# A fused kernel of a state-space block and an FP4 feed-forward: VectorE's order within a turn

## The chip, the cores and the metric

The kernel runs on one core of a Trainium2 chip, in one launch. The metric is the device time in microseconds (us). The core's engines are TensorE (PE, with its weight loads PEld), VectorE (DVE), ScalarE (ACT), GpSimd (POOL) and SyncE (SP, which here only issues transfers). Each runs its own instruction list in order; they meet through semaphores.

## What is computed

With `x` of 2 x 4096 tokens by 512 channels, the result is the sum of `x`, a state-space block and a feed-forward whose operands are quantized to FP4:

```python
xn = layernorm(x)
# state-space block on xn
y  = xn + ssm_scan(rmsnorm(xn, scale1), A, B, C, D)
a  = y + gelu(rmsnorm(y, scale2) @ w1 + b1) @ w2 + b2
# feed-forward on the same xn; q() is blockwise FP4, 16 values to a scale
gate = q(xn) @ q(w_gate).T
up   = q(xn) @ q(w_up).T
f    = q(silu(gate) * up) @ q(w_down).T
out  = x + a + f
```

The hidden width of the feed-forward is 1408 (11 blocks of 128), that of the GELU layer 2048. `q` divides each block of 16 values by its scale, rounds the magnitudes to the eight FP4 values, and multiplies by the scale again.

## The kernel before, in words

Tokens come in 64 tiles of 128, joined to 32 pairs of tiles. A matrix product is done as three passes (high by high, high by low, low by high), for full fp32 accuracy.

**Three stages.** A head (about 0 to 115 us) quantizes and turns the first weights and inputs. Then 179 **turns** of the feed-forward follow, up to about 1780 us (`window(s)`, for s from 1 to `NW` = 179, written out for each engine). Then comes the MLP stage of the GELU layer (`mlp1`, `mlp2`, `gelu_parts`) up to the end. The hidden values of one turn (one hidden block of 128 for two pairs of tiles, 128 partitions by 512) are called group s.

**What a turn does with a group.** In turn s TensorE forms gate(s) and up(s) (`gu_half`, line 752), 12 matmuls each, and down(s-2) (`down`, line 774), 12 matmuls. ScalarE takes SiLU of gate(s) into the one buffer `sg` (line 1326). Everything else of turn s is about group s-1, a chain across three engines: VectorE multiplies `sg` by up's bank (`h_mult`, line 957), turns 32x32 blocks so that the 16-value blocks lie along the row (`h_rows`, line 965), reduces and inverts the scales (`front`: lines 992, 1003, 997); GpSimd multiplies by the inverse (`scaled`, line 1527); ScalarE takes magnitudes (line 1291); VectorE rounds in two passes (`mid_a` and `mid_b`, lines 1009 and 1017); GpSimd multiplies by the scale (`dequant`, line 1533); VectorE turns the blocks back (`h_back`, line 971); ScalarE rounds to the high part (line 1319) and GpSimd subtracts it (`h_low`, line 1541). down(s-1) reads that in turn s+1.

**The order by hand.** Each engine's list is written out. The waits that matter here: up(s) may overwrite its bank only after `h_mult(s-1)` (line 751, semaphore `s_hm`); gate(s) only after SiLU(s-1); SiLU(s) may overwrite `sg` only after `h_rows(s-1)` (line 1325); `h_mult(s)` waits for SiLU(s) and up(s) (lines 955 and 956); `down(s)` waits for `h_low(s)` (line 767). On VectorE, `h_mult(s-1)` is the first step of turn s, and `h_back(s-1)` all but the last.

**Side work in a turn.** In some turns VectorE also quantizes another tile (a "side job", `SIDE`): `x_norm` (line 978), which waits for a load, and `front` in one turn, `mid_a`/`mid_b` in the next, and an `x_turn` (line 1032) behind `h_back` two turns after that. Others have statistics (`stats`), sums of finished output tiles (`z_add`, line 1119), taps of the state-space kernel (turns 11 to about 65) or the state-space matmuls (`ssm_*`, turns 99 to 162).

**The normed tiles.** From turn 164 (`PRE0`) on, the first four tiles of the MLP stage are prepared in three steps each (`prepare(t, part)`): part 0 is `tile_add` (lines 1181 and 1185; it waits for the loads of lines 570 and 574), part 1 `tile_root` (lines 1191, 929 to 945, and 1197), part 2 `tile_low` (line 1212). On VectorE parts 1 and 2 stand ahead of the rounding passes, part 0 behind the turn's last step. SP issues the loads of tile 0 behind its turn 163, those of tile t+1 behind TensorE's `h_turn(t)` (line 857). GpSimd adds two sums to each tile (`tile_z`, lines 1618 and 1621), the second behind part 0. In turns 176 to 179 VectorE also splits weights (`w_low`, line 1176), behind `h_back`.

Of the kernel before, what the change touches and what calls it, by code (L numbers as in the profile page):

```python
# [24 lines left out]
NW = NP // 2 * NF + LAG  # L25
NV = 32
NB = NT // 4
SW = 1
# [3 lines left out]
PRE0 = 164  # L32
# [16 lines left out]
def last(n):  # L49
    return first(n) + NF - 1  # L50
# [39 lines left out]
def side(s):  # L90

    return JOF[SIDE[s]] if s in SIDE else None


def prompt(m):

    return SWIN[JOBS[m]] < NF


def h_job(s):  # L100

    return JOF["h", s - 1] if SW <= s <= NW else None
# [31 lines left out]
def plan_slice(s):  # L134

    def upto(s):
        if s < UW0:
            return 0 if s < SW else min(s, 4) if s < 8 else min(s - 3, NT - 4)
        return NT - 4 + min(NT, 2 * (s - UW0 + 1))
    return range(upto(s - 1) if s else 0, max(upto(s), upto(s - 1) if s else 0))  # L140
# [18 lines left out]
def job_width(m):  # L159
    kind, i = JOBS[m]  # L160
    if kind == "h":
        return 2 * P * len(pairs(i))
    return CW[(i - 22) // 4] if kind == "w" and i >= 22 else 512


def build(nc, x, A, B, C, Dv, sc1, sc2, w1, b1, w2, b2, wg, wu, wd, cst, out):
# [12 lines left out]
    with ExitStack() as ctx:  # L179
# [735 lines left out]
        def vector_program(e):  # L915
# [37 lines left out]
            def h_mult(w):  # L953
                n = job_width(JOF["h", w])
                e.wait_ge(s_sg, w + 1)
                e.wait_ge(s_gu, w + 1)
                e.tensor_tensor(sg[:, 0:n], UB_[:, 0:n], sg[:, 0:n], ALU.mult).then_inc(s_hm, 1)  # L957

            def h_rows(w):

                m = JOF["h", w]
                n = job_width(m)
                wait_qa(e, m)
                e.wait_ge(s_hm, w + 1)
                e.transpose(qa[:, m % 4, 0:n], sg[:, 0:n]).then_inc(s_src, 1)  # L965

            def h_back(w):
                m = JOF["h", w]
                n = job_width(m)
                e.wait_ge(s_ph, m + 1)  # L970
                e.transpose(qb[:, m % 2, 0:n], qa[:, m % 4, 0:n]).then_inc(s_t2, 1)  # L971
# [9 lines left out]
            def biggest(m):  # L981
                n = job_width(m)
                s_ = qs[:, m % 4, 0, 0:n // 16]
                if JOBS[m][0] == "w" and m < NJ:
                    e.wait_ge(d_xin[NLOAD[m] % 4], 16 * (NLOAD[m] // 4 + 1))
                elif JOBS[m][0] == "w":
                    e.wait_ge(d_xs[place(m)], 16 * loads(m))
                else:
                    e.wait_ge(s_src, NSOURCE[m])
                if m >= 4:  # L990
                    e.wait_ge(s_ph, m - 3)
                e.tensor_reduce(s_, blk(job_in(m)), AX, ALU.max, apply_absolute_value=True).then_inc(s_mx, 1)  # L992

            def inverse(m):
                nb = job_width(m) // 16
                e.wait_ge(s_sc, m + 1)
                e.reciprocal(qs[:, m % 4, 1, 0:nb], qs[:, m % 4, 0, 0:nb]).then_inc(s_rc, 1)  # L997

            def front(m):
                s_ = qs[:, m % 4, 0, 0:job_width(m) // 16]  # L1000
                biggest(m)
                e.wait_ge(s_mx, m + 1)
                e.tensor_scalar(s_, s_, 1.0 / 6.0, 1e-12, ALU.mult, ALU.max).then_inc(s_sc, 1)
                inverse(m)
# [14 lines left out]
            def low(m):  # L1019
                nk = job_width(m) // P  # L1020
                hi, lo = job_dst(m)
                tin = turned(m).rearrange("p (k c) -> p k c", c=P)
                e.wait_ge(s_hi, TPOS[m])
                e.tensor_tensor(lo, tin, hi.bitcast(F32), ALU.subtract).then_inc(s_lo, 1)  # L1024

            def x_turn(m):

                n = JOBS[m][1] // 2
                e.wait_ge(d_xb[place(m)], 64 * returns(m))
                if n >= 3:  # L1030
                    e.wait_ge(s_gu, last(n - 3) + 1)
                e.transpose(whole(m), xin[:, place(m)].rearrange("p (k c) -> p k c", c=P)).then_inc(s_xt, 1)
# [69 lines left out]
            def ssm_scan(v, h):  # L1102
                w = 2 * v + h
                e.wait_ge(s_e, 2 * v + 2)
                if w:
                    e.wait_ge(s_sb, w)
                else:
                    e.wait_ge(d_a128, 16 * 32)
                    e.wait_ge(d_uo[0], 16 * 8)
                    e.wait_ge(d_uo[1], 16 * 8)  # L1110
                for k in range(4):
                    ins = e.tensor_tensor_scan(sS[:, k, :], a128[:, w:w + 1].to_broadcast([P, 32]),
                                               SSB[0][:, P * h + 32 * k:P * h + 32 * k + 32], 0.0, ALU.mult, ALU.add)
                ins.then_inc(s_scan, 1)

            def z_add(t):
                e.wait_ge(s_dn, last(t // 2) + 1)
                e.wait_ge(d_xr[t % 2], 16 * (t // 2 + 1))
                e.tensor_tensor(xin[:, 2 + t % 2], DNB[t % 4][:], xin[:, 2 + t % 2], ALU.add).then_inc(s_z, 1)
# [3 lines left out]
            def window(s):  # L1123
                k = s - S0
                h, x_ = h_job(s), side(s)
                fronted, low_x = side(s - 1), side(s - 3)
                outputs = 0 <= k < 2 * NV and k % 2
                h_mult(s - 1)
                if low_x in TPOS:
                    low(low_x)  # L1130
                elif low_x is not None and prompt(low_x):
                    x_turn(low_x)
                h_rows(s - 1)
                front(h)
                if outputs:
                    ssm_scan(k // 2, 0)
                for n in range(NP):
                    if s == last(n) + 3:
                        z_add(2 * n)
                        z_add(2 * n + 1)  # L1140
                for n in plan_slice(s):
                    kind, t = LATER[n]
                    if kind == "bn":
                        stats(t)
                    if kind == "bn" and t + 1 == ROOTS[rooted(t) - 1][1]:
                        todo.extend(batch_rsqrt(rooted(t) - 1))
                for step in todo[0:6 if s < 14 else 3]:
                    step()
                del todo[0:6 if s < 14 else 3]
                if PRE0 <= s < PRE0 + 12 and (s - PRE0) % 3 == 1:  # L1150
                    prepare((s - PRE0) // 3, 1)
                if PRE0 + 3 <= s < PRE0 + 15 and (s - PRE0) % 3 == 0:
                    prepare((s - PRE0) // 3 - 1, 2)
                if outputs:
                    ssm_scan(k // 2, 1)
                if fronted is not None:
                    mid_a(fronted)
                    mid_b(fronted)
                mid_a(h)
                mid_b(h)  # L1160
                if s in (K0 - 2, K0 - 1):
                    kernel_heads(s - K0 + 2)
                if x_ is not None:
                    if SIDE[s][0] == "x":
                        x_norm(x_, place(x_), lambda: e.wait_ge(d_xs[place(x_)], 16 * loads(x_)))
                    front(x_)
                h_back(s - 1)
                if low_x in XPOS and not prompt(low_x):
                    x_turn(low_x)
# [47 lines left out]
            def prepare(t, part):  # L1217
                if t < NT:
                    (tile_add, tile_root, tile_low)[part](t)
# [21 lines left out]
            for m in range(NJ + 2):  # L1241
                if m < NJ:
                    if HEAD[m][0] == "x":
                        x_norm(m, m % 4, lambda: e.wait_ge(d_xin[NLOAD[m] % 4], 16 * (NLOAD[m] // 4 + 1)))
                    biggest(m)
                if m >= 2:
                    mid_a(m - 2)
                if m < NJ:
                    inverse(m)
                if m >= 2:  # L1250
                    mid_b(m - 2)
                if m < 2:
                    stats(2 * m)
                    stats(2 * m + 1)
                if m == 1:
                    steps.extend(batch_rsqrt(0))
                for step in steps[0:2]:
                    step()
                del steps[0:2]
            for s in range(SW, NW + 1):  # L1260
                window(s)
                if PRE0 <= s < PRE0 + 12 and (s - PRE0) % 3 == 0:
                    prepare((s - PRE0) // 3, 0)
                if 0 <= s - (NW - 3) < 4:
                    w_low(s - (NW - 3))
            gelu_parts(0)
# [438 lines left out]
```

## Time and profile before

| | |
|---|---|
| median of 3 runs | 3181.51 us (3181.39 to 3181.73) |
| the profiled execution | 3186.95 us |
| its span | 3185.2 us |
| TensorE busy | 3076.3 us, 97% |
| VectorE busy | 2016.9 us, 63% |
| ScalarE, GpSimd busy | 1090.9 us, 1152.1 us |

All rows come from one profiled execution; its own time is 5.4 us above the median, and 1.75 us of it lie outside the span. A row of the timeline gives start, duration, engine, line, operation, the tiles written and read with their shapes, the count of merged instructions, and in square brackets the idle time of the engine just before, with what ended it. For merged rows the duration is that of the whole run.

### The profile page before, as it was taken

To read this page: it belongs to the slowest core of one execution; us is meant where nothing else is said; L and a number is where in the kernel's file an instruction comes from. 1 tells how busy PE (TensorE), PEld (TensorE's weight loads), DVE (VectorE), ACT (ScalarE), POOL (GpSimd) and SP (SyncE) were. 2 spreads that over 40 slices of the span, in tenths; PEclk is the share of its full clock that TensorE was granted. 3 is DMA by queue.
4 is the path that set the end of the run, shared out by engine and by line. 5 is a ranking of instruction groups with operands and counts; after the bars stand their busy time and mean duration, and the time that the engine had idled before them with its cause. 6 is when DMAs were issued, how large, how long until landed. Compare 5 with 4: busy or idle time off the path is not lost.

```text
span 3185.2 us, 43122 instructions
## 1 busy us (share of the span) xinstructions
PE 3076.3 (97%) x14861; PEld 2470.3 (78%) x14861; DVE 2016.9 (63%) x4427; ACT 1090.9 (34%) x1910; POOL 1152.1 (36%) x1097
## 2 busy tenths in 40 slices
PE   5799999999999999999999999999999999999999
PEld 2578777777777777777777788888888888888887
DVE  7788888887777666766777654444454544454442
ACT  5435655545444333334332322121222121122121
POOL 7555556555555545555554211110111111111100
PEclk9999999999999999999999999999999999999999
DMA  4133333347766665666643533333333333333320
GB/s 119 47 87 90 111 118 90 107 119 178 186 175 161 160 166 144 157 161 176 159 117 91 136 70 72 74 71 78 65 80 73 70 71 74 71 70 75 71 59 15
DMA packets 865577, 335.58 MB, mean 105 GB/s; under 512 B 680400, under 2 KB 771792, under 8 KB 862800
## 3 DMA queue, kind: packets, MB, share of 16 engines
q1 hardware_dynamic: 865360, 332.83, 42.8%
q8 instruction: 119, 1.95, 0.2%
q14 instruction: 98, 0.80, 0.1%
HBM read 225.21 MB, written 107.51 MB: 104 GB/s over the span
## 4 chain that ended last, share of the span: by engine, by line
PE 64%; DVE 18%; issue 6%; POOL 4%; ACT 3%; DMA 2%; SPq 2%; DVEq 0%; ACTq 0%; POOLq 0%
PE bank L874 22%; PE bank L890 22%; PE bank L752 11%; PE bank L774 5%; DVE qs L992 3%; POOL qa L1533 3%; DVE qa L1009 2%; DVE qa L965 2%; DVE sg L957 2%; PE bank L815 2%; DVE qb L1017 2%; POOL qa L1527 1%; ACT ub L1378 1%; PE bank L823 1%; DVE qb L971 1%
## 5 line engine op out<-in xcount | busy, mean ns | idle before, releaser
L874 PE MATMUL bank<-hT,Wp 128*128 128x512 f32 x3072 | 743.6, 391 | 2.1 <-DVE Wp L1176 1.6
L890 PE MATMUL bank<-Wp,G 128*128 128x512 f32 x3072 | 743.8, 391 | 0.0
L874 PEld LDWEIGHTS bank<-hT,Wp 128*128 128x128 f32 x3072 | 576.4, 188 | 127.8 <-issue 2.0
L890 PEld LDWEIGHTS bank<-Wp,G 128*128 128x128 f32 x3072 | 576.6, 188 | 126.2
L752 PE MATMUL bank<-XT,Wu 128*128 128x512 f32 (+1 forms) x2148 | 522.3, 392 | 39.7 <-DVE sg L957 38.5
L752 PE MATMUL bank<-XT,Wg 128*128 128x512 f32 (+1 forms) x2148 | 525.5, 394 | 12.8 <-DVE Wd L1024 5.8
L774 PE MATMUL bank<-Wd,HT 128*128 128x512 f32 x2112 | 514.0, 392 | 0.4 <-POOL HT L1541 0.4
L752 PEld LDWEIGHTS bank<-XT,Wu 128*128 128x128 f32 x2148 | 397.7, 190 | 147.5 <-issue 68.2
L1225 DVE CAST G<-gf 128x512 fp32r<-128x512 f32 x256 | 110.3, 431 | 607.5 <-PE bank L890 588.4
L752 PEld LDWEIGHTS bank<-XT,Wg 128*128 128x128 f32 x2148 | 398.5, 190 | 103.0 <-issue 14.6
L774 PEld LDWEIGHTS bank<-Wd,HT 128*128 128x128 f32 x2112 | 393.7, 188 | 94.0 <-issue 12.3
L1533 POOL TENSOR_TENSOR qa<-qb,qs 128x512 f32<-128x512 f32 (+2 forms) x277 | 306.7, 1108 | 319.2 <-DVE qb L1017 316.8
L1479 ACT ACTIVATE gf<-bank,vec 128x512 f32<-128x512 f32 x256 | 176.2, 688 | 613.8 <-PE bank L874 613.8
L1527 POOL TENSOR_TENSOR qa<-qa,qs 128x512 f32<-128x512 f32 (+1 forms) x243 | 263.2, 1083 | 209.3 <-DVE qs L997 209.3
L1618 POOL TENSOR_TENSOR zx<-zl,b2r 128x512 f32<-128x512 f32 x64 | 86.7, 1355 | 615.2 <-DMA out_dram<-zx 532.3
L1541 POOL TENSOR_TENSOR HT<-qb,HT 128x512 fp32r<-128x512 f32 (+1 forms) x179 | 229.7, 1283 | 194.4 <-ACT HT L1319 194.4
L1621 POOL TENSOR_TENSOR zx<-zx,xl 128x512 f32<-128x512 f32 x64 | 82.9, 1295 | 515.4 <-DVE xl L1185 515.3
L1319 ACT ACTIVATE HT<-qb 128x512 fp32r<-128x512 f32 (+1 forms) x179 | 112.1, 626 | 381.0 <-DVE qb L971 380.9
L971 DVE STREAM_TRANSPOSE qb<-qa 128x512 f32<-128x512 f32 (+1 forms) x179 | 122.0, 682 | 137.6 <-POOL qa L1533 137.6
L1227 DVE TENSOR_TENSOR G<-gf,G 128x512 fp32r<-128x512 f32 x256 | 186.2, 728 | 8.8
L1326 ACT ACTIVATE sg<-bank 128x512 f32<-128x512 f32 (+1 forms) x179 | 105.9, 591 | 244.5 <-PE bank L752 198.9
L1009 DVE SCALAR_TENSOR_TENSOR qa<-qb,qa 128x512 f32<-128x512 f32 (+2 forms) x149 | 116.1, 779 | 93.3 <-ACT qb L1291 93.0
(114 smaller groups left out, 2840.4 us busy)
## 6 DMA issues: line engine op xcount, KB each, us to landing
px<-in_L_attn_x_dram SPq DMA_DIRECT2D x128, 256.0 KB, 3.2
xin<-in_L_attn_x_dram SPq DMA_DIRECT2D x128, 256.0 KB, 3.4
sT<-r_K SPq DMA_DIRECT2D x128, 256.0 KB, 4.1
r_Z<-xin SPq DMA_DIRECT2D x64, 256.0 KB, 2.3
r_U<-ub SPq DMA_DIRECT2D x16, 1024.0 KB, 6.6
sU<-r_U SPq DMA_DIRECT2D x32, 512.0 KB, 5.4
r_Y<-sY SPq DMA_DIRECT2D x16, 1024.0 KB, 5.5
xl<-in_L_attn_x_dram SPq DMA_DIRECT2D x64, 256.0 KB, 3.1
```

The lines of the kernel that those rows point to most:

```text
L752: ins = e.matmul(bk[:, 0:n], W[wh][:, k, :], inputs(xh, w, k), start=(k == 0 and p_ == 0), stop=(k == KD - 1 and p_ == 2))
L774: ins = e.matmul(DNB[t % 4][:], HT[hh][:, w % 2, a * P:(a + 1) * P], Wd[wh][:, f, :], start=(w == first(n) and p_ == 0), stop=(w == last(n ...
L874: ins = e.matmul(bk[:], Wp[f][wh][:, 0, k * P:(k + 1) * P], hT[xh][b % 2][:, k, :], start=(k == 0 and p_ == 0), stop=(k == KD - 1 and p_ = ...
L890: ins = e.matmul(ACC[j][:], G2[gh][:, n % 2, j * P:(j + 1) * P], Wp[f][wh][:, 1, :], start=(f == 0 and p_ == 0), stop=(f == 15 and p_ == 2))
L971: e.transpose(qb[:, m % 2, 0:n], qa[:, m % 4, 0:n]).then_inc(s_t2, 1)
L1009: e.scalar_tensor_tensor(Aa, Bb, FLOOR, Aa, ALU.max, ALU.add).then_inc(s_t, 1)
L1227: e.tensor_tensor(G2[1][:, n % 2], gf[:, n % 2], G2[0][:, n % 2].bitcast(F32), ALU.subtract).then_inc(s_glo, 1)
L1319: e.activation(HT[0][:, w % 2, 0:n], qb[:, m % 2, 0:n], ACT.Copy).then_inc(s_hh, 1)
L1479: e.activation(gf[:, n % 2], PB[n % 2][:], ACT.Gelu, bias=vec[:, f:f + 1]).then_inc(s_gl, 1)
L1527: e.tensor_tensor(blk(qa[:, m % 4, 0:n]), blk(job_in(m)), bc(qs[:, m % 4, 1, 0:n // 16], n // 16), ALU.mult).then_inc(s_pa, 1)
L1533: e.tensor_tensor(blk(qa[:, m % 4, 0:n]), blk(qb[:, m % 2, 0:n]), bc(qs[:, m % 4, 0, 0:n // 16], n // 16), ALU.mult).then_inc(s_ph, 1)
L1541: e.tensor_tensor(lo, qb[:, m % 2, 0:n], hi.bitcast(F32), ALU.subtract).then_inc(s_hl, 1)
```

## The change

On VectorE alone:

- `h_mult(s)` moves from the first step of turn s+1 to a place ahead of `h_back(s-1)` in turn s. So the product of the next group comes before the last group is turned back. The product of group 0 stands ahead of the loop.
- Part 0 of a normed tile moves from behind the turn to the place where parts 1 and 2 stood; parts 1 and 2 move behind the rounding passes (and behind a side job's `x_norm` and `front`), just ahead of the product.

```diff
--- before.py
+++ after.py
@@ -1125,7 +1125,6 @@
                 h, x_ = h_job(s), side(s)
                 fronted, low_x = side(s - 1), side(s - 3)
                 outputs = 0 <= k < 2 * NV and k % 2
-                h_mult(s - 1)
                 if low_x in TPOS:
                     low(low_x)
                 elif low_x is not None and prompt(low_x):
@@ -1147,10 +1146,8 @@
                 for step in todo[0:6 if s < 14 else 3]:
                     step()
                 del todo[0:6 if s < 14 else 3]
-                if PRE0 <= s < PRE0 + 12 and (s - PRE0) % 3 == 1:
-                    prepare((s - PRE0) // 3, 1)
-                if PRE0 + 3 <= s < PRE0 + 15 and (s - PRE0) % 3 == 0:
-                    prepare((s - PRE0) // 3 - 1, 2)
+                if PRE0 <= s < PRE0 + 12 and (s - PRE0) % 3 == 0:
+                    prepare((s - PRE0) // 3, 0)
                 if outputs:
                     ssm_scan(k // 2, 1)
                 if fronted is not None:
@@ -1164,6 +1161,12 @@
                     if SIDE[s][0] == "x":
                         x_norm(x_, place(x_), lambda: e.wait_ge(d_xs[place(x_)], 16 * loads(x_)))
                     front(x_)
+                if PRE0 <= s < PRE0 + 12 and (s - PRE0) % 3 == 1:
+                    prepare((s - PRE0) // 3, 1)
+                if PRE0 + 3 <= s < PRE0 + 15 and (s - PRE0) % 3 == 0:
+                    prepare((s - PRE0) // 3 - 1, 2)
+                if s < NW:
+                    h_mult(s)
                 h_back(s - 1)
                 if low_x in XPOS and not prompt(low_x):
                     x_turn(low_x)
@@ -1257,10 +1260,9 @@
                 for step in steps[0:2]:
                     step()
                 del steps[0:2]
+            h_mult(SW - 1)
             for s in range(SW, NW + 1):
                 window(s)
-                if PRE0 <= s < PRE0 + 12 and (s - PRE0) % 3 == 0:
-                    prepare((s - PRE0) // 3, 0)
                 if 0 <= s - (NW - 3) < 4:
                     w_low(s - (NW - 3))
             gelu_parts(0)
```

No instruction is added or removed, and the lists of the other engines stay as they are.

## Rows read from the trace of the kernel before

**Rows 1.** The page: busy time, share of the span, instructions.

```profile
PE 3076.3 (97%) x14861; PEld 2470.3 (78%) x14861; DVE 2016.9 (63%) x4427; ACT 1090.9 (34%) x1910; POOL 1152.1 (36%) x1097
```

**Rows 2.** The busy time by stretch (start:end and length, then PE, PEld, DVE, ...).

```profile
1900.00:3185.00 1285.00, 1281.87 (x5610) 1052.48 (x5608) 598.74 (x1562) 253.18 (x565) 140.81 (x107) 1.00 0.33 68
```

**Rows 3.** TensorE's waits, whole span: total us, times, longest.

```profile
PE bank L752 <- DVE sg L957: 38.5, 43, 2.9
...
PE bank L752 <- issue: 4.5, 2, 2.7
```

**Rows 4.** The same view by stretch: 200 to 1010, then 1640 to 1785 us.

```profile
PE bank L752 <- DVE sg L957: 21.0, 30, 1.6
...
PE bank L752 <- DVE sg L957: 10.4, 9, 2.9
```

**Rows 5.** Timeline, a turn in which VectorE waits ahead of turning back.

```profile
415.32 0.69 DVE L1017 SCALAR_TENSOR_TENSOR qb<-bank,qa 128x512 f32<-128x512 f32 x1
...
416.09 1.06 POOL L1533 TENSOR_TENSOR qa<-qb,qs 128x512 f32<-128x512 f32 x1 [1.65 <-DVE qb L1017]
417.18 0.71 DVE L971 STREAM_TRANSPOSE qb<-qa 128x512 f32<-128x512 f32 x1 [1.17 <-POOL qa L1533]
...
418.41 0.65 DVE L957 TENSOR_TENSOR sg<-bank,sg 128x512 f32<-128x512 f32 x1
...
418.64 1.29 POOL L1541 TENSOR_TENSOR HT<-qb,HT 128x512 fp32r<-128x512 f32 x1 [1.49 <-ACT HT L1319]
...
419.21 2.98 PE L752 MATMUL bank<-XT,Wu 128*128 128x512 f32 x12 [0.64 <-DVE sg L957]
...
422.02 2.91 PE L774 MATMUL bank<-Wd,HT 128*128 128x512 f32 x12
```

**Rows 6.** Timeline, a turn with a side job ahead of turning back.

```profile
426.67 0.66 DVE L971 STREAM_TRANSPOSE qb<-qa 128x512 f32<-128x512 f32 x1
...
427.24 0.65 DVE L957 TENSOR_TENSOR sg<-bank,sg 128x512 f32<-128x512 f32 x1
```

**Rows 7.** Timeline, TensorE rows released by the product.

```profile
123.57 1.66 PE L752 MATMUL bank<-XT,Wu 128*128 128x256 f32 x12 [0.45 <-DVE sg L957]
...
216.40 3.00 PE L752 MATMUL bank<-XT,Wu 128*128 128x512 f32 x12 [1.03 <-DVE sg L957]
...
1237.06 4.38 PE L752 MATMUL bank<-XT,Wu 128*128 128x512 f32 x12 [2.93 <-DVE sg L957]
...
1761.79 2.49 PE L752 MATMUL bank<-XT,Wu 128*128 128x256 f32 x12 [2.93 <-DVE sg L957]
```

**Rows 8.** Timeline, a load waited for, and TensorE released by GpSimd's last subtraction.

```profile
1233.90 0.55 DVE L978 TENSOR_SCALAR qa<-xin,mv,rst 128x512 f32<-128x512 f32 x1 [6.17 <-DMA xin<-in_L_attn_x_dram]
...
966.55 3.02 PE L774 MATMUL bank<-Wd,HT 128*128 128x512 f32 x12 [0.37 <-POOL HT L1541]
```

**Rows 9.** Timeline, normed tile 0: scales, add, product, then steps of the root.

```profile
1643.92 0.35 DVE L997 RECIPROCAL qs<-qs 128x32 f32<-128x32 f32 x1
...
1650.51 0.86 DVE L1181 TENSOR_SCALAR xl<-xl,mv,rst 128x512 f32<-128x512 f32 x1
...
1652.01 0.68 DVE L957 TENSOR_TENSOR sg<-bank,sg 128x512 f32<-128x512 f32 x1
...
1655.09 0.10 DVE L1191 TENSOR_SCALAR rs<-rs 128x1 f32<-128x1 f32 x1
...
1655.26 1.06 POOL L1527 TENSOR_TENSOR qa<-qa,qs 128x512 f32<-128x512 f32 x1 [0.51 <-DVE qs L997]
1655.42 0.91 DVE L933 TENSOR_TENSOR rs<-rs 128x1 f32<-128x1 f32 x1
...
1657.92 0.49 DVE L1197 TENSOR_SCALAR xl<-xl,rs 128x512 f32<-128x512 f32 x1
```

**Rows 10.** Line 574 from 1643.5 to 1645 us: tile 0's second load alone.

```profile
L574 SPq DMA_DIRECT2D yl<-r_Y x1: 1907/1907/1907, 1643.0 to 1643.0; - x1
DMA to landing us min/median/max: 5.1/5.1/5.1
```

## The prediction

> **What bounds the kernel now.** I read the page first: TensorE is busy for 97% of the span and VectorE for 63% [rows 1]. So TensorE sets the time, and only its idle time of 3185.2 - 3076.3 = 109 us can be won. The busy time by stretch comes next: from 1900 us to the end TensorE is busy for 1281.87 of 1285 us [rows 2], so the MLP stage holds nothing, and the change doesn't touch it. TensorE's waits then say who ends the idle time: the largest item is the product of gate and up, line 957, with 38.5 us in 43 waits of at most 2.9 us [rows 3]. That is the wait of up(s) for the product of group s-1, which the change moves. Most of the rest lies in the head ahead of the turns, where there is no product yet. By stretch the 38.5 us are 21.0 in the turns from 200 to 1010 us (30 waits) and 10.4 in the last turns (9) [rows 4]; of the other four, two lie between, in the state-space stage, with 2.93 each (the later one at 1237.06), and two in the first turns, with 1.2 together [rows 7].
>
> The timeline shows what VectorE does ahead of such a product, and there are two kinds. **Kind A**: VectorE ends its second rounding pass at 416.01, waits 1.17 us for GpSimd's scale, turns the group back, does another turning, and starts the product at 418.41; TensorE had stood for 0.64 us [rows 5]. I count 25 of these, the first at 216.40 and the last at 1761.79 [rows 7], 22.8 us together: 16 of them with 12.4 us in the stretch of 21.0, all nine of the stretch of 10.4. **Kind B**: a side job fills that wait, so turning back starts at once and the product 0.57 us behind it [rows 6]. These are 18, first 123.57 and last 1237.06 [rows 7], with 38.5 - 22.8 = 15.7 us.
>
> **The change part by part.** No instruction is added or removed.
>
> *The product ahead of turning back.* In kind A it can start at about 416.05 in place of 418.41, 2.3 us earlier, since its up(s) ended long before (TensorE is already standing ahead of up(s+1)). Its 0.65 us then lie in the 1.17 us in which VectorE waited for GpSimd, so the turning back isn't later, and the next turn's chain starts about 0.6 us earlier. The longest wait of kind A before 1640 us is 1.6 us, under 2.3, so all 16 go: 12.4 us. In kind B the product comes 0.57 us earlier and nothing else does: turning back slips by 0.6 us, `h_rows` stays. Cut by 0.57 at most, the 14 of kind B from 200 to 1010 us (8.6 us in all, seven of them above 0.57) give 7 x 0.57 + 2.4 = 6.4 us.
>
> *What comes back.* Where two such turns follow each other, the second wait grows by what the first lost, because VectorE's own chain is no faster through a turn of kind B: four such places, some 1.3 us. At 202.95 and 233.30 us gate waits with no releaser named (4.5 us, rows 3), and there GpSimd's subtraction of a turned tile ends just before it; that hangs on VectorE's chain, not on the product, and takes back about 0.7 us of what two earlier waits lose. The 1.2 us of the first two turns I take as lost again, since TensorE next waits there for VectorE's low part of a weight. So the stretch to 1010 us gives 12.4 + 6.4 - 1.3 - 0.7 = 16.8 us.
>
> *The two waits of 2.93 us in the state-space stage* are of kind B with a load in front: VectorE stood 6.17 us for an input tile [rows 8]. The load's time stays; each gives 0.57, together 1.1 us.
>
> *Normed tiles.* Gross there are 10.4 us [rows 4]. Against them stands the new order. Part 0 of tile 0 now comes when VectorE gets past its scales, at 1643.92 + 0.35 = 1644.3 [rows 9], but the second load lands only at 1643.0 + 5.1 = 1648.1 [rows 10]. So VectorE stands 3.8 us with the rounding passes of both a side job and the group behind it; GpSimd's scale, ScalarE's high part and TensorE's down wait behind those. By my count the product of that turn then ends at about 1653.1, where it ended at 1652.01 + 0.68 = 1652.7 before [rows 9], and the next turn's chain starts 1.3 us late. For tiles 1 to 3 the load costs 0 to 3 us, mostly in slack. The root takes 1655.09 to 1658.41, 3.3 us [rows 9]. Before it lay partly in VectorE's wait for ScalarE's magnitudes; now it stands bare ahead of the product, and only the 1.1 us of GpSimd's scale cover it for the turning back. So in each of the four turns with a root the product is about as late as before, and behind `tile_add` GpSimd's two sums meet its subtraction. The low part (1.1 us) fits under the scale. Won is the 1.5 us that `tile_add` stood ahead of the product (1650.51 to 1652.01, rows 9). Following the eleven turns row by row, I get between 1 us and 4 us for them and the last turns with `w_low`, where the product no longer stands behind the weight split (2.93 us at 1761.79, rows 7). Bounds: all 10.4 at best; at worst 3 us lost, a wait of 1.8 more in each root turn. I take 2, near the row count.
>
> *The product beside GpSimd.* It now runs while GpSimd scales. The trace has no such pair for line 957, but a two-input pass with one operand in PSUM, 415.32, takes 0.69 us [rows 5], the shortest of such passes; I take 0. The bound is 1.06 us, GpSimd's own duration, from below 0.
>
> *The rule on ports.* A root step of one element that started 0.16 us behind GpSimd's 1.06 us took 0.91 us [rows 9]; a few more of the moved steps now meet GpSimd. The Trainium skill, SBUF — State Buffer, section Who interferes with whom, says that VectorE's instructions with two SBUF inputs, and its two-port modes, exclude GpSimd's reads for their whole length, either way round. By that rule both parts of `tile_add` would also meet the scaling with the inverse, up to 1.06 us in each of four turns, and the sum would be 16 us in place of 20. By that rule also the product, with one operand in PSUM, stays free; no row of it shows the contrary.
>
> **The sum.** 16.8 + 1.1 + 2 = 19.9, say 20 us. The profiled execution would take 3186.95 - 20 = 3167.0; the median of the runs stands 5.4 us lower, so 3161.5 us.
>
> *The clock* I leave out of the sum. Behind the waits of 2.93 us the twelve matmuls of up took 4.38 us [rows 7], and 2.98 us behind one of 0.64 [rows 5]. If the shortened 2.35 us don't bring that, up to 1.4 us more are won at each; 2.35 lies between the two rows, nearer to the longer, so I count nothing.
>
> **Rivals.**
> (1) *All product waits go*, if TensorE's lead never meets another wait, and the clock stays up: 38.5 us, 3143 us. For it: 2.3 us of room in kind A. Against: kind B gains only 0.57, loads and roots stay. 10%.
> (2) *The next wait takes over.* down(s-1) needs GpSimd's subtraction, which ended at 418.64 + 1.29 = 419.93, 2.1 us ahead of down at 422.02 [rows 5]; as TensorE gets earlier, this room shrinks, and once it was already used up (0.37 us at 966.55, rows 8). With the turned tiles of `x_turn` it is the same. Half of the 17.9 us before 1640 comes back, and the normed tiles give nothing: 9 us, 3172.5 us. 20%.
> (3) *Slower: the product holds the turning back.* `h_back` now stands behind a product that waits for up(s). Where VectorE is ahead of TensorE, the group is turned back only 0.65 us after up(s) ends, then ScalarE, GpSimd and down(s-1) follow. It decides from the point at which turning back is later than the 2.1 us of room. ScalarE's magnitudes come behind SiLU(s), which needs gate(s), so the passes end close to the end of up(s) and nothing should be held. Were it 0.25 us beyond the room in each of the 179 turns, 45 us would come and 20 go: 3206 us. 6%.
> (4) *No measurable change*, if roots and load waits (up to 3 us a tile) eat what is won: within 6.4 us, 3180. 8%.
> The forecast, a gain of 14 to 28 us, has the remaining 56%.
>
> **How the numbers follow.** A measurement can tell about 0.2% (6.4 us) from no change. Faster is the forecast with (1) and (2), 86%; same (4), 8%; slower (3), 6%. The range goes from 3146 us (a gain of 35, short of rival 1) to 3174 us, with most of rival 2 inside; outside are the far end of (1), (3) and (4), not quite 2 in 10.
>
> **What would show it.** TensorE's wait for line 957 falls from 38.5 to about 15 us: near 0 for turns without a side job, about 2.35 twice, 1 to 2 in root turns. VectorE's wait for line 1533 ahead of line 971 (1.17 each) shrinks to about 0.5. A new wait of 3 to 4 us for `yl` stands ahead of line 1185 at tile 0. Rival 2 would show as waits for line 1541 or with no releaser; rival 3 as VectorE idle ahead of line 957 for TensorE's line 752 in most turns. The forecast is wrong if the product's waits go and the time doesn't follow.

## The result, and the profile after

The changed kernel takes **3164.52 us** (median of 4 runs, 3164.18 to 3165.86) against 3181.62 (4 runs, 3181.39 to 3182.23): ratio 0.9939, 95% interval 0.9927 to 0.9952. By the medians that is 17.1 us less, by the ratio 19 us; the time is 3 us above the forecast of 3161.5 and inside its range.

The page of after, against [rows 1]:

```profile
span 3162.4 us, 43122 instructions
PE 3064.0 (97%) x14861; PEld 2470.7 (78%) x14861; DVE 2046.9 (65%) x4427; ACT 1088.3 (34%) x1910; POOL 1147.0 (36%) x1097
```

The span is 22.8 us shorter: 10.5 us of TensorE's idle time are gone (108.9 to 98.4) and 12.3 us of its busy time. VectorE is 30 us *busier*, with the same instructions. TensorE's waits over the turns, against [rows 3]:

```profile
PE bank L752 <- DVE sg L957: 16.8, 19, 2.2
PE bank L752 <- DVE Wd L1024: 6.3, 4, 2.3
PE bank L774 <- POOL HT L1543: 6.0, 7, 1.4
PE bank L815 <- DVE sS L1112: 5.3, 6, 1.1
PE bank L752 <- issue: 5.2, 2, 3.4
```

The product (line 957) gave up 21.7 of its 38.5 us. Some 12 us of waits came back at other places, though: before, the low part (line 1543, 1541 before) had 0.4 us in one wait, the state-space scan's copy (line 1112) 0.4 in two, `Wd` 5.8 in four, and the waits with no releaser 4.5 [rows 3 for the last]; the waits behind the feed-forward turns add 0.5. By stretch it is now 6.3 us in 11 waits from 200 to 1010 us, and 5.6 us in 5 from 1640 to 1785 [against rows 4].

Sorted by whether turn s-1 has a side job, the waits of up(s) for the product are these. Kind A (no side job) went from 22.8 us in 25 waits to 6.1 in 6, and none of the six comes before turn 165. Kind B went from 15.7 us in 18 to 10.7 in 13.

To see where the time comes from I compare the start of up(s), turn by turn, and call the difference the **lead** over before. It is 6.8 us at turn 28, 16.8 at turn 61, 24.1 at turn 102, 24.0 at turn 161, 25.1 at turn 177 (1761.79 [rows 7] less 1736.70), and 22.8 at the end. So the gain is made in the plain feed-forward turns, nothing moves in the state-space stage, and the end gives 2.3 back. The lists of TensorE's waits hold only part of it. Of the 24.0 us from turn 0 to turn 102, 13.9 are idle time and 10.1 are *busy* time. In 60 of these turns neither kernel has a listed wait, and they gained 6.7 us; the other 42 gained 17.3 us, where their listed waits fell by 13.3. Gaps under 0.15 us, which no list shows, can't be the difference: they sum to 1.2 us before and 0.7 after. Nor can the clock: the granted clock is 1.00 in this stretch in both kernels. The rest stands in the matmul records, whose ends are modelled. The weight loads (PEld) show it, as in turn 51 before:

```profile
560.97 2.57 PEld L752 LDWEIGHTS bank<-XT,Wu 128*128 128x128 f32 x12 [0.54 <-issue]
561.00 2.96 PE L752 MATMUL bank<-XT,Wu 128*128 128x512 f32 x12
```

The matmuls have no wait, but their weight load stood 0.54 us until the product's end (560.86). The turn took 8.57 us before and 8.16 after, where that idle time is gone. Over the whole run the idle time of these loads with no releaser ("issue") fell from 68.2 to 26.5 us.

What VectorE did with the cover. The turn of [rows 5] is now:

```profile
408.76 0.68 DVE L957 TENSOR_TENSOR sg<-bank,sg 128x512 f32<-128x512 f32 x1
408.93 1.06 POOL L1535 TENSOR_TENSOR qa<-qb,qs 128x512 f32<-128x512 f32 x1 [1.65 <-DVE qb L1017]
410.02 0.71 DVE L971 STREAM_TRANSPOSE qb<-qa 128x512 f32<-128x512 f32 x1 [0.57 <-POOL qa L1535]
```

The product lies in GpSimd's scale, and of VectorE's wait of 1.17 us ahead of turning back 0.57 are left. Over the whole run, first that wait, before and after (total, times, longest), then the scale step, line 1003, before and after (out<-in, count, busy us, mean ns, idle before).

```profile
DVE qb L971 <- POOL qa L1533: 137.6, 114, 2.2
```

```profile
DVE qb L971 <- POOL qa L1535: 55.7, 106, 1.6
```

```profile
L1003 DVE TENSOR_SCALAR qs<-qs 128x32 f32<-128x32 f32 x234 | 49.3, 211 | 8.1
```

```profile
L1003 DVE TENSOR_SCALAR qs<-qs 128x32 f32<-128x32 f32 x234 | 96.5, 413 | 8.1
```

VectorE saves 81.9 us of waiting, and pays 47.2 us of it back in an instruction that nobody touched. Of its 234 executions 13 took over 0.35 us before, 98 after. The turn of [rows 6] shows why; the first two rows are of before, the others of after:

```profile
428.06 1.30 POOL L1541 TENSOR_TENSOR HT<-qb,HT 128x512 fp32r<-128x512 f32 x1 [0.17 <-ACT HT L1319]
...
429.47 0.18 DVE L1003 TENSOR_SCALAR qs<-qs 128x32 f32<-128x32 f32 x1
```

```profile
418.70 0.63 DVE L957 TENSOR_TENSOR sg<-bank,sg 128x512 f32<-128x512 f32 x1
419.24 0.70 DVE L971 STREAM_TRANSPOSE qb<-qa 128x512 f32<-128x512 f32 x1
419.86 0.67 DVE L965 STREAM_TRANSPOSE qa<-sg 128x512 f32<-128x512 f32 x1
420.57 0.69 DVE L992 TENSOR_REDUCE qs<-qa 128x32 f32<-128x512 f32 x1
420.69 1.29 POOL L1543 TENSOR_TENSOR HT<-qb,HT 128x512 fp32r<-128x512 f32 x1 [0.77 <-ACT HT L1321]
421.29 0.73 DVE L1003 TENSOR_SCALAR qs<-qs 128x32 f32<-128x32 f32 x1
422.05 0.35 DVE L997 RECIPROCAL qs<-qs 128x32 f32<-128x32 f32 x1
```

The product no longer stands between turning back and the blocks of the next group. Before, the scale step started 2.80 us behind the start of the turning back (426.67, rows 6), 0.11 us after the end of GpSimd's low part. Now it starts 2.05 us behind, while GpSimd makes the low part of the last group, which begins 1.45 us behind the turning back and lasts 1.29. It ends at 422.02, as GpSimd's instruction does (421.98). The search for the maxima, beside the same instruction, takes its usual 0.69 us. This is the exclusion that the prediction weighed for other instructions. The Trainium skill (SBUF — State Buffer, Who interferes with whom) has VectorE's second port pair shared with GpSimd under an exclusive lock; the trace agrees, with 0.18 us free and 0.73 us beside it.

### The profile page after: what moved, and what is told of

Read it like the earlier page. It is cut to its first block, busy times and chain, and to the rows that moved or that the text cites. A ratio compares the mean times of both kernels' runs of the same rounds, so it can differ in the third digit from the quotient of the medians.

```text
span 3162.4 us, 43122 instructions
## 1 busy us (share of the span) xinstructions
PE 3064.0 (97%) x14861; PEld 2470.7 (78%) x14861; DVE 2046.9 (65%) x4427; ACT 1088.3 (34%) x1910; POOL 1147.0 (36%) x1097
## 4 chain that ended last, share of the span: by engine, by line
PE 69%; DVE 14%; issue 5%; POOL 4%; DMA 3%; SPq 2%; ACT 2%; DVEq 0%; POOLq 0%; ACTq 0%
PE bank L874 22%; PE bank L890 22%; PE bank L752 14%; PE bank L774 7%; DVE qs L992 2%; POOL qa L1535 2%; DVE qa L1009 2%; PE bank L815 2%; DVE qs L1003 1%; DVE qa L965 1%; DVE qb L1017 1%; POOL qa L1529 1%; PE bank L823 1%; PE bank L722 1%; SPq L493 1%
## 5 line engine op out<-in xcount | busy, mean ns | idle before, releaser
L752 PE MATMUL bank<-XT,Wu 128*128 128x512 f32 (+1 forms) x2148 | 513.6, 388 | 17.1 <-DVE sg L957 16.8
L752 PEld LDWEIGHTS bank<-XT,Wu 128*128 128x128 f32 x2148 | 399.8, 189 | 106.9 <-issue 26.5
L992 DVE TENSOR_REDUCE qs<-qa 128x32 f32<-128x512 f32 (+1 forms) x243 | 165.2, 680 | 8.3
```

The lines of the kernel that those rows point to most:

```text
L752: ins = e.matmul(bk[:, 0:n], W[wh][:, k, :], inputs(xh, w, k), start=(k == 0 and p_ == 0), stop=(k == KD - 1 and p_ == 2))
```

## The experiments

Ratios are against the kernel before on the same chip (3184 to 3186 us there); "worth" is the ratio's difference from 1 times 3182 us. no_cover, side_turns, plain_turns, side_last, low_later and rows_too are built on product_only; steps_only, product_first and add_behind on the changed kernel. The cuts of code are shortened: the product of group 0 ahead of the loop and lines that only move are left out, and the remarks behind # are not in the kernels.

**Does a repeat read the same?** One run of the kernel before, unchanged, and the changed kernel again.

> The kernel before, unchanged, for a second profile of it. Theory 1 (the profile of before was a usual one): its span again stands some 3.7 us above the median of the runs, and TensorE waits again 38 to 39 us for the product. Theory 2 (that execution was slow by 5 us somewhere): a span of about 3180 us, and the places where the two profiles of the same kernel differ hold the 5 us; then part of the 22.8 us between the two spans is not the change's.

> The changed kernel, unchanged, beside the others on this chip. Both theories: 0.994 of before (0.993 to 0.995), and its profile again shows about 17 us of product waits, 6 us of waits of down for GpSimd's subtraction and 5 us of the state-space outputs for the scan.

The kernel before took 3187.73 us, product waits 39.0 us in 41, lead never over 1 us at the turns named above. The changed kernel took 3164.01 us, ratio 0.9935 (0.9923 to 0.9948), lead 23.8 at turn 102 and 25.5 at turn 177. So the first profile of before was a usual one, and at these turns two executions of one kernel agree to about 1 us; over the whole span the changed kernel's two profiles are 1.6 us apart. Between kernels it can be more. product_only (below) has the changed kernel's order up to turn 163, and leads by 20.2 us at turn 102, not 24; its profiled execution was the slowest of its five. So a difference of under 4 us between the leads of two kernels tells nothing; what a lead gains between two turns of one execution is read below, to about 1 us.

**The two parts of the change alone.** product_only moves the product and leaves the steps of the normed tiles; steps_only does the reverse.

```diff
-                h_mult(s - 1)            # first step of turn s
+                if s < NW:               # ahead of h_back(s - 1)
+                    h_mult(s)
```

> Only the product is moved; the steps of the normed tiles stay where they were. Theory 1 (the product makes the gain, the steps' move gives nothing or costs a little): 3161 to 3164 us, as fast as the changed kernel or up to 3 us faster, and TensorE's waits for GpSimd's subtraction (line 1543) of the last turns are gone. Theory 2 (the steps' move is worth its own 2 us or more): 3167 us or more.

> Only the steps of the normed tiles are moved; the product stays the first step of a turn. Theory 1: 3180 to 3186 us, no faster than before: what the add no longer holds up, the root now holds up, since it stands bare behind the rounding passes. Theory 2 (the steps are worth something by themselves): 3174 to 3178 us.

product_only: 3160.73 us, ratio 0.9924 (0.9911 to 0.9936), worth 24 us. steps_only: 3192.34 us, 1.0017 (1.0008 to 1.0026), a loss of 5 us; its lead falls from 0.9 at turn 161 to -7.0 at turn 177. The product carries the whole gain. That the steps cost some of it rests on steps_only, whose interval lies above 1, and on the leads; the intervals of product_only and the changed kernel overlap.

**What in the product's move pays?** no_cover keeps the new order and takes the cover away; VectorE waits for GpSimd's scale first:

```diff
                 if s < NW:
+                    e.wait_ge(s_ph, JOF["h", s - 1] + 1)
                     h_mult(s)
```

> Product alone moved, as in product_only, but VectorE first waits for GpSimd's scale, so that the product stands ahead of turning back and is no longer covered by that wait. Theory 1 (in turns without a side job half of the gain comes from the cover: the product starts 1.2 us later than in product_only and every chain through such a turn is 0.65 us longer): gain of 9 to 14 us of the 24, that is 3172 to 3177 us where before is 3186. Rival (the order alone makes the gain, for most waits are under 0.7 us): 20 us or more.

It was slower than before: 3195.45 us, ratio 1.0035 (1.0023 to 1.0048), where I expected a gain. The timeline of no_cover: the wait has moved to the product, with the turning back behind both, and in the next turn (last row) the scale step is blocked as in after.

```profile
417.74 0.69 DVE L957 TENSOR_TENSOR sg<-bank,sg 128x512 f32<-128x512 f32 x1 [1.17 <-POOL qa L1536]
418.35 0.70 DVE L971 STREAM_TRANSPOSE qb<-qa 128x512 f32<-128x512 f32 x1
...
429.62 0.73 DVE L1003 TENSOR_SCALAR qs<-qs 128x32 f32<-128x32 f32 x1
```

Line 1003 is blocked 98 times of 234, as in after, so the new order by itself is worth less than nothing (-11 us). The whole gain hangs on the 0.65 us of VectorE's work that lie in GpSimd's time.

**Which turns pay?** side_turns moves the product only in turns with a side job, plain_turns only in the others.

```diff
-                if s < NW:
+                if s < NW and x_ is not None:     # side_turns; plain_turns: x_ is None
                     h_mult(s)
...                                   # in the other turns h_mult(s - 1) opens the turn, as before
```

> The product ahead of turning back only in turns with a side job (kind B); in all others it stays the first step of the next turn. Theory 1 (worth 0.57 us at most where a product is waited for): gain of 4 to 8 us. Rival (all turns gain alike): 8 to 12 us.

> Built on product_only: the product goes ahead of the turning back only in turns without a side job; in the others it stays where it was. side_turns, its counterpart, lost 8 us against before. If the two edits simply add (product_only gained 24 us, side_turns lost 8 to 9), this gives 3150 to 3156 us. If the gain in the plain turns needs the order in the side-job turns as well (a lead is carried from turn to turn), it gives 3170 to 3185 us. In either case the waits for L957 of the plain turns go and those of the side-job turns (some 18 of 30) stay: 12 to 20 us of them.

side_turns: 3192.81 us, ratio 1.0027 (1.0017 to 1.0038), 9 us *slower*. plain_turns: **3152.96 us**, ratio 0.9899 (0.9885 to 0.9912), 32 us faster than before and the best kernel of the study, ahead of the changed one by 12 us. The two simply add: -32 + 9 = -23 against product_only's -24. In a turn with a side job `x_norm` and `front` fill GpSimd's time already [rows 6], so the product there pushes the turning back out by 0.6 us, and the scale step into the low part (53 of 234 blocked in side_turns, 59 in plain_turns, 13 before). How the 9 us divide between these two, no run separates. TensorE's waits for the product in side_turns show where they land:

```profile
PE bank L752 <- DVE sg L957: 41.3, 45, 2.9
```

Kind B fell as it should, from 15.7 us in 18 waits to 7.9 in 8, but kind A, the waits of the other turns, grew from 22.8 us in 25 to 33.3 in 37. TensorE's waits in plain_turns:

```profile
PE bank L752 <- DVE sg L957: 11.4, 12, 3.0
PE bank L774 <- POOL HT L1545: 6.6, 10, 2.0
```

Kind A is gone but for 0.2 us. Kind B holds the other 11.2 us, in 11 waits, against 15.7 in 18 before. Up to turn 102 that is 6.5 us with the side-job turns as they were, and 6.3 in the changed kernel, which moves their product too. So moving it there doesn't shorten kind B any further; what shortens it in both kernels is the faster chain of the plain turns.

**Other places.** product_first puts the product right behind the rounding passes, ahead of the side job; side_last is product_only with the side job behind the turning back.

```diff
+                if s < NW:               # product_first: ahead of x_norm and front
+                    h_mult(s)
                 if x_ is not None:
```

> As the changed kernel, with the product still earlier: ahead of a side job's x_norm and front, and of the moved steps. Theory 1 (in turns with a side job the product gained only 0.57 us because it stands behind the side job, and the two waits of 2.2 us are those for a load): the product waits fall from 16.8 to under 4 us, and the time to 3152 to 3157 us. Rival (the chain behind the product sets the pace, not the product): the product waits go and come back as waits for line 1543 or without a releaser, and the time stays at 3161 to 3166 us.

> As product_only, with the side job's x_norm and front behind turning back, at the end of the turn. Theory 1 (product_first lost because turning back stood behind product and side job, so that down waited for GpSimd's subtraction): product waits under 3 us and waits for line 1543 under 5 us, and the time 3 to 8 us under product_only. Rival (VectorE's whole chain through a turn with a side job is the bound: 1.9 us of side job now cover nothing, and rows come later by the 0.5 us that was covered): as slow as product_only or slower, with waits for SiLU or the product back.

product_first: 3172.43 us, ratio 0.9957 (0.9944 to 0.9969), slower than either theory said; of the rival the part holds that the waits come back at line 1543. side_last: 3194.27 us, ratio 1.0031 (1.0019 to 1.0043), slower than product_only, as the rival said, so theory 1 fell; the waits are at line 1543, which neither said. Waits of product_first, then of side_last:

```profile
PE bank L774 <- POOL HT L1543: 21.1, 27, 2.6
```

```profile
PE bank L774 <- POOL HT L1543: 36.9, 39, 2.8
```

In both TensorE waits for the low part instead: the wait of rival 2 appears as soon as VectorE's side work is put where the next group or the turning back has to wait for it.

**Is it the low part that blocks line 1003?** low_later has GpSimd make the low part behind the scaling of the next group; rows_too leaves GpSimd alone and moves the next group's turning (line 965) ahead of the turning back as well.

```diff
-                if s - 2 >= SW - 1:      # low_later, GpSimd
-                    h_low(s - 2)
                 scaled(h)
+                if s - 2 >= SW - 1:
+                    h_low(s - 2)
```

```diff
                     h_mult(s)            # rows_too, VectorE
+                    h_rows(s)            # no longer at the start of turn s + 1
                 h_back(s - 1)
```

> Built on product_only: GpSimd makes the low part of the last group (L1543) behind the scaling of the next one (L1529) instead of ahead of it. The theory of the blocked step says: L1003 then meets no work of GpSimd, its mean falls from 428 to about 200 ns; the chain of the turns gets 0.5 us shorter or more, but the low part comes 1.5 to 2.5 us later, so that TensorE's waits for it (HT, 7.8 us in 13 waits in product_only) grow by at least 20 us: 3170 to 3200 us in all, with the waits for L957 near nothing. If L1003 stays above 350 ns, the low part is not what blocks it, and the theory falls.

> Built on product_only (3160.73 us): the next group's rows into blocks (L965) also move ahead of the turning back, right behind the product, so that both lie beside GpSimd's rounding sum, and the search for the maxima follows the turning back directly. The theory of the blocked step says: of the 0.65 us that the moved product takes off the chain, about 0.5 us is eaten because the scale step (L1003) now comes while GpSimd makes the low part of the previous group (L1543); in product_only L1003 means 428 ns against 211 ns before. Here L1003 comes about 1.3 us after the start of the turning back, just ahead of that low part (+1.46 us), so its mean goes back to 180 to 260 ns, and the chain of a turn is 0.2 to 0.5 us shorter: 3150 to 3158 us, waits for the gelu product (L957) below 8 us. The rival, that what is left are fixed costs of the order (DVE in a row, no room), says no change against product_only (3158 to 3164 us) whatever L1003 takes. A third, that scaled (GpSimd) now waits for its own low part instead of for the scales, says L1003 short but the time the same, with GpSimd's L1529 without idle before it.

low_later: 3212.25 us, ratio 1.0083 (1.0069 to 1.0096). Its rows:

```profile
L1003 DVE TENSOR_SCALAR qs<-qs 128x32 f32<-128x32 f32 x234 | 43.5, 186 | 8.1
PE bank L774 <- POOL HT L1543: 56.3, 61, 2.1
```

Not one of the 234 is blocked, so the low part is the cause. Moving it is no cure: TensorE then waits 56.3 us for it, and the time is 12 us above the range expected. rows_too: 3160.62 us, ratio 0.9923 (0.9909 to 0.9937), the same as product_only. Its timeline:

```profile
425.96 0.18 DVE L1003 TENSOR_SCALAR qs<-qs 128x32 f32<-128x32 f32 x1
426.10 1.30 POOL L1544 TENSOR_TENSOR HT<-qb,HT 128x512 fp32r<-128x512 f32 x1 [1.55 <-ACT HT L1322]
426.17 0.35 DVE L997 RECIPROCAL qs<-qs 128x32 f32<-128x32 f32 x1
427.35 1.52 POOL L1530 TENSOR_TENSOR qa<-qa,qs 128x512 f32<-128x512 f32 x1
427.98 1.44 DVE L1017 SCALAR_TENSOR_TENSOR qb<-qb,qa 128x512 f32<-128x512 f32 x1
```

The scale step is short here (59 of 234 blocked over the whole run), and the inverse is ready at 426.52, but GpSimd is still at its low part and starts scaling only at 427.35. In product_only GpSimd waited for the inverse 206 times, here 108 times. That is the third theory of the expectation: GpSimd's low part stands in the chain either way, once as a block on VectorE, once on its own queue. The mean of line 1003 fell only to 368 ns, above the 180 to 260 expected, and the blocks it lost turn up elsewhere. GpSimd's scaling in the rows above took 1.52 us where 1.06 is usual, and VectorE's second rounding pass beside it 1.44 where it takes 0.69 by itself. The first rounding pass with both inputs in SBUF, in product_only and then in rows_too:

```profile
L1009 DVE SCALAR_TENSOR_TENSOR qa<-qb,qa 128x512 f32<-128x512 f32 x142 | 117.2, 826 | 116.1 <-ACT qb L1293 115.8
```

```profile
L1009 DVE SCALAR_TENSOR_TENSOR qa<-qb,qa 128x512 f32<-128x512 f32 x142 | 132.2, 931 | 123.0 <-ACT qb L1294 121.9
```

It pays 15.0 us more, while the scale step pays 14.0 less (100.1 to 86.1). How the missing gain divides between this and GpSimd's queue is not shown.

**What do the steps cost?** add_behind is the changed kernel with part 0 put back behind the turn.

> The changed kernel with one step put back: the sum of a normed tile (part 0) stands behind the turn again, parts 1 and 2 stay behind the rounding passes. Against product_only (3160.73 us) it moves parts 1 and 2 alone, against the changed kernel (3164.0 to 3164.5 us) part 0 alone. In steps_only and in the changed kernel VectorE waited for the copy of the sum's other input (yl) 2.5 us, three waits of 3.8 to 6.5 us in all, where before had none; the theory that this wait is what the moved steps cost says: the wait for yl is gone, the lead over before grows from turn 161 to turn 177 by 4 to 7 us, as in product_only (+5.8), not by 1 as in the changed kernel, and the time is 3157 to 3162 us. The rival, that parts 1 and 2 (a chain of short steps ahead of the product) are what costs, says a growth of 0 to 2 us and 3163 to 3168 us.

3164.75 us, ratio 0.9939 (0.9925 to 0.9952), and its lead goes from 24.2 at turn 161 to 24.3 at turn 177; product_only's grew by 5.8, the changed kernel's by 1.1. So my theory of the load fell, and the rival holds: it is parts 1 and 2. (Behind turn 177 product_only gives 3.5 us back, the other two 1.7 and 2.3.) The timeline of product_only, where the root's twelve steps (line 1192 is the first) stand ahead of the rounding passes:

```profile
1661.44 0.35 DVE L997 RECIPROCAL qs<-qs 128x32 f32<-128x32 f32 x1
1661.71 0.10 DVE L1192 TENSOR_SCALAR rs<-rs 128x1 f32<-128x1 f32 x1
1664.94 0.69 DVE L1009 SCALAR_TENSOR_TENSOR qa<-qb,qa 128x512 f32<-128x512 f32 x1
1666.27 0.68 DVE L957 TENSOR_TENSOR sg<-bank,sg 128x512 f32<-128x512 f32 x1
```

and of add_behind, where they stand behind them, as in the changed kernel:

```profile
1659.30 0.35 DVE L997 RECIPROCAL qs<-qs 128x32 f32<-128x32 f32 x1
1661.49 0.69 DVE L1009 SCALAR_TENSOR_TENSOR qa<-qb,qa 128x512 f32<-128x512 f32 x1 [1.84 <-ACT qb L1293]
1662.83 0.14 DVE L1192 TENSOR_SCALAR rs<-rs 128x1 f32<-128x1 f32 x1
1666.06 0.68 DVE L957 TENSOR_TENSOR sg<-bank,sg 128x512 f32<-128x512 f32 x1
1666.89 4.57 PE L752 MATMUL bank<-XT,Wu 128*128 128x512 f32 x12 [1.83 <-DVE sg L957]
```

From the inverse to the product it is 4.83 us in the first and 6.76 in the second, 1.9 more: the root's 3.2 us stood in the 1.84 us in which VectorE waits for ScalarE's magnitudes anyway. Behind the passes they stand bare, and TensorE waits 1.83 us.

## Why the prediction was right, point by point

The mechanism is the one forecast, for kind A. The number is close in part by luck: two terms of the sum were off in opposite directions, and the step from the profile to the median was off against their sum. The sum said 19.9 us; the two profiled spans are 22.8 us apart, the two medians 17.1. The profile of before stood 5.4 us above its median, that of after 0.3 below, and the prediction took 5.4 for both.

- **The bound, and the place of the gain.** Right: TensorE's waits for line 957, in the turns to 1010 us; the MLP stage holds nothing.
- **Kind A, 12.4 us.** The mechanism is right, shown by no_cover: the product hides in GpSimd's time (VectorE's mean wait ahead of turning back fell from 1.21 to 0.53 us), and without the cover nothing is won. All 16 waits went, as forecast. The size was low: plain_turns, which has it alone, leads by 27.5 us at turn 102. The term summed the listed waits, but TensorE also stood where its rows show it busy (10.1 of the 24.0 us above), and kind B's waits shrink too as the chain gets faster.
- **Kind B, 6.4 us.** Wrong in sign. The step that failed is "the product comes 0.57 us earlier and nothing else does: turning back slips by 0.6 us", with nothing charged for that slip. side_turns has a lead of -6.0 us at turn 102. The cut itself came as forecast: kind B's waits up to there fell from 9.8 to 3.7 us. But kind A's rose from 12.4 to 22.7, which fits a chain that starts later in the turn behind. The low part, which slips with the turning back, and the scale step, which runs into it, were there to price.
- **The sum to 1010 us, 16.8.** Measured 24.1 (turn 102). The two errors partly cancelled: the parts alone give 27.5 - 6.0 = 21.5.
- **State-space stage, 1.1 us.** Measured -0.1 from turn 102 to 161, and +1.2 in the repeat. Both long waits did shrink (2.93 to 2.19 and 2.20 us), and the clock gave 3.0 us more (below), but in these turns TensorE waits 4.2 us more for VectorE's line 1112, which the prediction left out. In plain_turns that is 0.6 us more, and the stage gains 2.9.
- **Normed tiles, 2 us.** Measured +1.1 from turn 161 to 177 (+0.5 in the repeat), and -2.3 behind it: down waits there for the low part, 1.15 and 1.00 us. The wait for `yl` was foreseen at 3.8 us, and stood at 2.56 (line 1188, at 1624.53); the root turns wait 1.31, 1.33, 1.28 and 0.96 us, where 1 to 2 were foreseen. The loss of the root ahead of the product was named, and add_behind shows that it is the larger part: parts 1 and 2 take back nearly all of the 5.8 us that the product alone wins there.
- **Ports.** The rule was charged to `tile_add` and to the root's steps. Where it mattered was a 0.2 us instruction that the change doesn't touch but shifts. "Every instruction behind a moved one meets other neighbours" was the missing step: some 85 more blocks of about 0.5 us. That the product itself is not slowed is right within 12 ns: its mean is 663 ns, 651 before.
- **Rivals.** (1) did not come: 16.8 us of product waits stay, close to the 15 foreseen. (2) came in part: 5.6 us more at the low part, where it said 9 (in product_first and side_last it came in full), while the gain in the other turns was larger than I had it. (3) did not come: VectorE waits for up ahead of the product 4.2 us in 19 times. (4) did not come.

## What to carry to other kernels

Before you move an instruction into another engine's time, check in which turns that time is still empty: moved in those alone, this product won 32 us in place of 24, and in the others it lost 9. Then walk the instructions *behind* it and see what each will run beside on GpSimd; a short step that a GpSimd pass blocks, as the scale step here, costs the rest of that pass. A string of tiny dependent steps belongs where the engine waits anyway, ahead of the wait's end and not behind it.

## What was not expected of the hardware

**A blocked instruction is booked as busy.** Line 1003 does the same work in 0.18 or 0.73 us, so VectorE's busy time rose by 30 us (before 2016.9) while it waited less. A mean that doubles between two kernels is the sign to look for.

**The clock does not go by the length of the wait.** Twelve matmuls of up took 4.58 and 4.38 us behind waits of 2.93 before, 3.00 and 2.97 us behind 2.19 and 2.20 after, but 4.57 us behind 1.83 in add_behind and 2.96 us behind 3.00 in plain_turns:

```profile
1207.14 2.96 PE L752 MATMUL bank<-XT,Wu 128*128 128x512 f32 x12 [3.00 <-DVE sg L957]
```

The granted clock in these two stretches (start:end, length, then PE busy, PEclk, DMA share, GB/s), add_behind first:

```profile
1666.90:1671.40 4.50, 4.50 (x13) 0.62 0.00 0
```

```profile
1207.20:1210.00 2.80, 2.80 (x12) 1.00 0.09 30
```

0.62 is mostly the lower level of 1.2 GHz, 1.00 the upper of 2.4. The changed kernel gained 3.0 us at the two long waits, where the granted clock was 0.62 and 0.66 before and 1.00 after. In the last turns the clock cancels: before, up and down of turn 177 took 2.49 and 3.67 us behind the wait of 2.93 (granted clock 0.60 in up; its row is in rows 7), after 1.67 and 3.03 behind one of 0.70 (1.00). Against that, twelve matmuls of the MLP stage (line 874, 1780.56) took 4.53 us behind a wait of 2.13 (0.63), where they took 3.01 behind 1.58 (1.00). What decides between the levels for waits of 1.8 to 3 us, no run here tells.

What stays open: whether plain_turns, which leaves the normed tiles' steps as they were before, would go below 3153 us with the scale step out of the low part's way was not tried; low_later and rows_too show two ways that move the cost instead.
